# Adding all mixture outputs on VectorE ahead of the first scan, and writing the skip term with ScalarE

## What is computed

```python
x = x + 0.5 * moe(LN(x))        # 8 experts, 2 chosen per token, hidden 512
x = x + mamba(LN(x)) + mamba'(flip(LN(x)))   # two directions, own weights
x = x + 0.5 * moe(LN(x))

def step(h, inp):                # per token t, channel d (256), state n (16)
    u_t, d_t, b_t, c_t = inp
    dA = jnp.exp(d_t[:, :, None] * A)
    h = h * dA + (d_t * u_t)[:, :, None] * b_t[:, None, :]
    return h, jnp.einsum('bdn,bn->bd', h, c_t)
y = scan(step) + xc * Dp         # xc * Dp is the skip term
y = (y * silu(z)) @ out_w.T
```

## Time and profile before

| | us |
|---|---|
| median of 3 runs | 2886.86 |
| lowest, highest | 2885.48, 2887.90 |
| the profiled execution | 2884.83 |
| its span, first to last instruction | 2883.0 |
| first mixture, 0 to 510 | 510 |
| between the mixture and the first scan, 510 to 558 | 48 |
| scan stage, 558 to 2323 | 1765 |
| second mixture and end, 2323 to 2883 | 560 |

### The profile page before, as it was taken

The page is one execution under the profiler, slowest core; times in us unless marked ns, Lnnn a source line. Parts: engine busy times, 40 slices in busy tenths (PEclk is TensorE's granted clock), DMA queues, the critical chain, the costliest instruction groups (busy, mean ns, idle before and its releaser), DMA issues.

```text
span 2883.0 us, 38519 instructions
## 1 busy us (share of the span) xinstructions
PE 2461.9 (85%) x11100; PEld 1556.7 (54%) x11100; DVE 2456.1 (85%) x3745; ACT 1583.6 (55%) x2776; POOL 2305.3 (80%) x1392
## 2 busy tenths in 40 slices
PE   4799999588898889889889889989988865999993
PEld 2699999343444444344344444434434435999993
DVE  6766666499999999999999999999999978666666
ACT  3355555466566566656656665665665541555551
POOL 1577777399999999999899999999998844777772
PEclk8899999899999999999999999999999987999996
DMA  7011112133333333233233333233323240111116
GB/s 226 14 49 49 49 49 49 61 101 100 97 106 103 96 106 101 92 107 102 94 105 106 97 103 106 95 100 107 100 92 99 97 136 5 45 49 49 49 49 192
DMA packets 159363, 254.75 MB, mean 88 GB/s; under 512 B 22114, under 2 KB 64002, under 8 KB 158594
## 3 DMA queue, kind: packets, MB, share of 16 engines
q1 hardware_dynamic: 140338, 209.21, 23.1%
q0 software_dynamic: 18464, 37.79, 4.9%
q10 hardware_dynamic: 432, 6.29, 0.5%
HBM read 219.65 MB, written 33.55 MB: 88 GB/s over the span
## 4 chain that ended last, share of the span: by engine, by line
DVE 29%; issue 21%; PE 16%; POOL 10%; ACT 5%; DMA 1%; POOLq 0%; DVEq 0%; SPq 0%
DVE buf L828 11%; PE bank L1342 7%; DVE bank L804 7%; DVE buf L819 6%; POOL buf L404 5%; ACT over L1069 2%; POOL token_outputs L414 2%; POOL buf L465 2%; PE bank L1338 2%; PE bank L1279 2%; PE bank L1287 2%; DVE buf L792 1%; PE bank L1193 1%; ACT L1035 1%; DVE X L727 1%
## 5 line engine op out<-in xcount | busy, mean ns | idle before, releaser
L465 POOL TENSOR_TENSOR buf<-buf 128x1024 f32<-128x1024 f32 x512 | 1203.4, 2362 | 140.0 <-DVE buf L828 114.8
L1342 PE MATMUL bank<-buf,id_sb 128*128 128x512 f32 x2048 | 1001.1, 618 | 105.8 <-POOL buf L465 100.8
L828 DVE TENSOR_TENSOR_SCAN buf<-over,bank 128x512 f32<-128x512 f32 x768 | 891.7, 1201 | 1.0
L1069 ACT ACTIVATE over<-wgu,negA 128x510 f32<-128x510 f32 x768 | 505.5, 711 | 470.4 <-DVE buf L828 429.8
L1342 PEld LDWEIGHTS bank<-buf,id_sb 128*128 128x128 f32 x2048 | 385.9, 195 | 538.9 <-issue 336.6
L804 DVE TENSOR_TENSOR bank<-wgu,bank 128x512 f32<-128x512 f32 x768 | 488.4, 681 | 6.6 <-PE bank L1329 4.1
L1212 PE MATMUL bank<-parts 128*128 128x256 f32 x3456 | 486.2, 291 | 3.2 <-issue 1.6
L1212 PEld LDWEIGHTS bank<-parts 128*128 128x128 f32 x3456 | 434.1, 192 | 7.1 <-issue 3.9
L414 POOL DMA_INDIRECT token_outputs<-buf,slot_out x288 | 292.8, 1017 | 110.2 <-issue 85.3
L404 POOL DMA_INDIRECT buf<-token_rows,slot_token x288 | 302.7, 1051 | 96.7 <-issue 90.4
L1329 PE MATMUL bank<-BCs,sel 104*128 104x512 f32 x384 | 271.9, 709 | 74.7 <-DVE bank L804 73.4
(11 more groups left out here) (158 smaller groups left out, 2403.0 us busy)
## 6 DMA issues: line engine op xcount, KB each, us to landing
buf<-state_rows SPq DMA_DIRECT2D x640, 256.0 KB, 3.2
token_rows<-buf SPq DMA_DIRECT2D x32, 256.0 KB, 2.3
y_pair<-token_outputs SPq DMA_DIRECT2D x16, 512.0 KB, 5.2
buf<-token_outputs SPq DMA_DIRECT2D x16, 512.0 KB, 5.0
buf<-token_rows,slot_token POOLq DMA_INDIRECT x288, 2.6
token_outputs<-buf,slot_out POOLq DMA_INDIRECT x288, 2.3
out<-X SPq DMA_DIRECT2D x16, 256.0 KB, 3.7
wgu<-wgT ACTq DMA_DIRECT2D x1, 2048.0 KB, 9.2
```

What stands on the lines that cost most here:

```text
L465: pool.tensor_tensor(hC[:, b, :].rearrange("p (c w) -> p c w", c=C), hs[:, b, :].rearrange("p (c w) -> p c w", c=C), Cs[:, b, :].unsqueeze ...
L828: V.tensor_tensor_scan(hs[:, b, w], dA[:, b, c, :, :].rearrange("p s t -> p (s t)"), bank[c], 0.0, ALU.mult, ALU.add).then_inc(s[f"scan_do ...
L1069: ins = A.activation(dA[:, n % R, c, :, 1:], delta[r][:, c * W:(c + 1) * W].rearrange("p (s t) -> p s t", s=S)[:, :, 1:], ACT.Exp, scale=n ...
L1342: ins = M.matmul(bank[4 + c], id_sb[:, :], hC[:, n % R, c * W:(c + 1) * W], start=False, stop=(n == NS - 1), skip_group_check=True)
```

## The change

Four things are changed.

- The loads of mixture outputs of all 16 groups of four tiles are made ahead of the first scan, eleven before SP's first store of B and C rows and five after it (`EARLY` = 11), into a ring of four buffers `y_pre`, which is the down weights' tile `wd_sb` under another shape.
- DVE adds them with the instruction that it uses after the second mixture, eight per group (`combine_early`): group 0, then pair 0's layer norm, groups 1 to 10, `split_lo(0, 0)`, groups 11 to 14, `step_size(0, 0)`, group 15 (`MIDDLE` = 15), and the first product. ACT's `scale_outputs` and POOL's `combine` are gone.
- The down weights are loaded a second time, at the end of unit 1, by SP.
- The skip term is written by ACT into the y banks at n = 2 of each unit, after the gate (`skip`, two instructions with Dp as the scale), and PE's first sum waits for it (`skip_done`) in place of the two skip products. Two products ahead of the first scan open the banks once (`y_opened`). `skip_sb` and `y_pair` are gone.

```diff
+EARLY, MIDDLE = 11, 15
+        y_pre = wd_sb[:, :, :].rearrange("p (b t k) d -> p b t k d", t=G, k=2)
...
             outputs_there(0)
-            sp.dma_start(y_pair[:, :, :, :], y_rows(0)).then_inc(s["y_pair_in"], DMA)
...
+            def load_early(g):
+                wait(sp, s["comb_done"], g - 3)
+                sp.dma_start(y_pre[:, g % 4, :, :, :], y_rows(g)).then_inc(s[f"y_pre{g % 4}"], DMA)
+
+            for g in range(EARLY):
+                load_early(g)
...
             store_rows(0, 0)
-            load_pair(1)
+            for g in range(EARLY, NG):
+                load_early(g)
...
+                        if u == 1 and n == NS - 1:
+                            sp.wait_ge(s["comb_done"], NG)
+                            sp.dma_start(wd_sb[:, :, :], wdT).then_inc(s["loaded_w"], DMA)
...
-            combine(0, 0)
-            combine(0, 1)
             rstd(0)
...
+            def combine_early(g):
+                dve.wait_ge(s[f"y_pre{g % 4}"], (g // 4 + 1) * DMA)
+                combine(0, g, y_pre[:, g % 4, :, :, :])
...
+            combine_early(0)
             layernorm(0)
+            for g in range(1, EARLY):
+                combine_early(g)
             split_lo(0, 0)
+            for g in range(EARLY, MIDDLE):
+                combine_early(g)
             step_size(0, 0)
+            for g in range(MIDDLE, NG):
+                combine_early(g)
             product(0, 0, 0)
...
+            def skip(u, r):
+
+                if isinstance(u, int) and u == 0:
+                    act.wait_ge(s["y_opened"], C)
+                wait(act, s["gated"], u)
+                act.wait_ge(s["act_pre"], done(ACT_PRE, f"xc1_{r}", u // 2))
+                for c in range(C):
+                    ins = A.activation(bank[4 + c], xc[r][:, c * W:(c + 1) * W], ACT.Copy,
+                                       scale=ch[:, r, c, DSK:DSK + 1])
+                ins.then_inc(s["skip_done"], 1)
...
+                        if n == ACT_AT["skip"]:
+                            skip(p * 2 + r, r)
...
                 if n == 0:
-                    wait(pe, s["gated"], p * 2 + r)
-                    for c in range(C):
-                        M.matmul(bank[4 + c], skip_sb[:, r, c, :], xc[r][:, c * W:(c + 1) * W],
-                                 start=True, stop=False, skip_group_check=True)
+                    pe.wait_ge(s["skip_done"], p * 2 + r + 1)
```

More of the change, by code:

```diff
@@ L43 @@
 DVE_AT = {"gate": 2, "stats": 5, "lo": 8, "size": 12}
-POOL_AT = {"first": 0, "second": 1, "rstd": 7, "du": 13}
-ACT_AT = {"silus": 4, "hi": 7, "res": 8, "parts": 10, "ln": 11, "xn": 12, "scale": 13, "xnT": 15}
+POOL_AT = {"rstd": 7, "du": 13}
+ACT_AT = {"skip": 2, "silus": 4, "hi": 7, "res": 8, "parts": 10, "ln": 11, "xn": 12, "xnT": 15}
 PE_AT = {"conv": 0, "z": 5, "xdbl": 6, "out": 7, "dt": 9, "xt": 13}
-SP_AT = {"pair": 3, "rows": 9}
+SP_AT = {"rows": 9}
+EARLY, MIDDLE = 11, 15
 NSTATE = 16
@@ L155, in macaron_kernel @@
         slot_token = sb("slot_token", [P, TILES * HT], I32)
-        y_pair = sb("y_pair", [P, G, 2, D])
         sel = sb("sel", [ROWS, BC], F32R)
@@ L344, in pair_rows @@
                             fetch_B(u, r, n + FETCH_B)
-                        if n == SP_AT["pair"] and r == 0 and not (last or isinstance(p, int) and p == NP - 2):
-                            load_pair(p + 2)
                         if n == SP_AT["rows"] and not (last and r == 1):
                             store_rows(u + 1, 1 - r)
+                        if u == 1 and n == NS - 1:
+                            sp.wait_ge(s["comb_done"], NG)
+                            sp.dma_start(wd_sb[:, :, :], wdT).then_inc(s["loaded_w"], DMA)
             store_rows(0, 0)
-            load_pair(1)
+            for g in range(EARLY, NG):
+                load_early(g)
             for n in range(FETCH_C):
@@ L475, in pair @@
                             product(p, r, n + MUL_LEAD)
-                        if r == 0 and not last:
-                            if n == POOL_AT["first"]:
-                                combine(p + 1, 0)
-                            if n == POOL_AT["second"]:
-                                combine(p + 1, 1)
-                            if n == POOL_AT["rstd"]:
-                                rstd(p + 1)
+                        if r == 0 and not last and n == POOL_AT["rstd"]:
+                            rstd(p + 1)
                         if n == POOL_AT["du"] and not (last and r == 1):
                             size_times_input(p + r, 1 - r)
-            def combine(p, k):
-                pool.wait_ge(s["y_scaled"], p + 1)
-                wait(pool, s["pair_added"], 2 * p + k)
-                pool.sem_inc(s["out_turn"], 1)
-                xt = X[:, bass.ds(p * G, G), :]
-                pool.tensor_tensor(xt, xt, y_pair[:, :, k, :], ALU.add).then_inc(s["pair_added"], 1)
             def size_times_input(p, r):
@@ L720, in moe, with combine @@
                 four(TILES // 4 - 1)
-            def combine(g, rows):
+            def combine(m, g, rows):
                 for k in range(2):
@@ L753, in _ @@
             chain(V.tensor_copy(dtp_parts[0][:, :, :], dtp_sb[:, :, :]))
[L754 to L758 removed]
+            V.tensor_tensor(dtp_parts[1][:, :, :], dtp_sb[:, :, :], dtp_parts[0][:, :, :].bitcast(F32),
+                            ALU.subtract).then_inc(s["parts_ready"], 1)
             for b in range(4):
@@ L1006, in normalise @@
                 ins.then_inc(s["act_norm"], 1)
-            def scale_outputs(p):
-                act.wait_ge(s["y_pair_in"], (p + 1) * DMA)
-                for t in range(G):
-                    for k in range(2):
-                        ins = A.activation(y_pair[:, t, k, :], y_pair[:, t, k, :], ACT.Copy,
-                                           scale=wt[:, k, p * G + t:p * G + t + 1])
-                ins.then_inc(s["y_scaled"], 1)
+            def skip(u, r):
[7 more added lines that the diff above has]
+                ins.then_inc(s["skip_done"], 1)
             def normT(p):
@@ L1108, in pair @@
                             log1pexp(pv, rv)
-                        if r == 1 and n == ACT_AT["scale"] and p + 2 < NP:
-                            scale_outputs(p + 2)
                         if r == 0 and not last:
@@ L1386, in _ @@
                          start=True, stop=True).then_inc(s["taps_spread"], 1)
+            for c in range(C):
+                M.matmul(bank[4 + c].rearrange("p (j d) -> p j d", j=G), ones_sb[:, :], id_sb[:, :].unsqueeze(1).broadcast_to([P, G, P]),
+                         start=True, stop=True).then_inc(s["y_opened"], 1)
             pe.wait_ge(s["taps_ready"], 1)
@@ L1392, in _ @@
             project_x(0, 0)
+            pe.wait_ge(s["parts_ready"], 1)
             project_dt(0, 0)
```

35 lines of the change are left out of this document (12 added, 23 removed).

## The result

| | us |
|---|---|
| before, median of 15 runs | 2885.75 |
| changed, median of 15 runs (lowest, highest) | 2891.65 (2889.47, 2893.35) |
| ratio, 95% interval | 1.0019 (1.0011 to 1.0027) |
| profiled span, before and after | 2883.0, 2888.4 |

The change costs 0.19%, where 2893.3 was forecast from a kernel of 2886.86 (ratio 1.0022): slower, by about as much as this kernel's measurement can tell from nothing. Two effects of opposite sign lie behind that.

What follows compares the result with a forecast made beforehand. DVE was taken to bound the scan stage, with nothing saturated ahead of the first scan. Profiled 2884.83 + 4.4 (start) + 2 (scan stage: -15 + 17) = 2891.2, or 2893.3 against the median of 2886.86; own range 2888 to 2901, wider 2875 to 2904.

Steps and rivals of the forecast that it cites:

- that case, 8 to 12 falls: Forecast's own case: 8 to 12 clock falls at the gates, start 2.6 to 8.2 us later, 2888 to 2901; chance 0.45.
- a start of +4.4: Ahead of the first scan: adds on DVE make the scans start 4.4 us later, bounds 2.6 to 8.2 us.
- not 0.50: At each gate: with the skip on ACT, PE's sums start 0.50 us earlier; -15 us over 30 gates, -20 to -8.
- six, not ten: PE's longer pause at the gates: 10 clock falls in 30, between 0 and 17; +17 us, between 0 and +30.
- predicted was +2: Scan stage as a whole: -15 us from the skip and +17 us from clock falls make +2 us.
- one wait of about 2 us at group 11: Sign ahead of the first scan: DVE busy from 521 us on, with this one wait, first product near 562.
- with group 15 beside POOL's product, in DVE's old wait: Before the first product: group 15 runs in DVE's old wait of 2.46 us; first product 3.7 us after `step_size` as before.
- an estimate of 6.6 us: Start if group 15 and POOL's product share a port and can't run side by side: 6.6 us later, not 4.4.
- What was taken at nothing: Scan stage: combine, scaling, second down-weights load (at most 3 us, once) and queued decay of state 6 at 0; end as before.
- the clock did not hold: Rival: the clock holds at the gates, so the skip's gain stands; 2876.3 us, chance 0.25.
- it did not fall at most gates: Rival: the clock falls at most gates, 17 falls costing 30 us; 2906.3 us, chance 0.12.
- a few falls only: Rival: five clock falls at the gates cost 9 us; 2885.3 us, no measurable difference, chance 0.18.

Runs made afterwards that it cites:

- the skip alone: The kernel before with only the skip term moved to ACT, the mixture adds left on POOL and ACT; ratio 0.9997.
- group 15 ahead: The changed kernel with group 15's adds on DVE ahead of `step_size` (`MIDDLE` = 16); ratio 1.0024 against the kernel before.
- the earlier loads: The changed kernel with 13 instead of 11 loads issued ahead of SP's first store of B and C rows; ratio 1.0015 against the kernel before.
- the skip on PE: The changed kernel with the skip term put back on PE, all 16 groups' adds staying on DVE; ratio 1.0024 against the kernel before.
- the zero product: The changed kernel with one product by a tile of zeros in PE's pause at the gate; ratio 0.999 against the kernel before.

## Why the prediction was right, point by point

The forecast was 2893.3 and the time is 2891.65, within the forecast's own range. The mechanisms were the ones named: a shorter chain, falls of the clock behind the longer pause, and a later start. But the condition of that case, 8 to 12 falls, did not come about; there were six. By the prediction's own prices (1.74 us for a fall) six falls and a start of +4.4 make 2886.9 - 15 + 10.4 + 4.4 = 2886.7, no measurable difference. The two terms were off by 2.6 and 4.5 us in opposite directions, so that the number came out within 2 us is in part luck.

**The skip on ACT.** ACT's pair takes 1.30 us (1.28 predicted) and the sums start 1.39 us behind the gate (1.38), where the earlier trace rows have 1.88. But the sums behind a pause reach their next instruction 3.54 us later (1129.32 to 1132.86), where behind no pause they take 3.43 (1134.79 to 1138.22), so 0.11 us is lost at once. The projection starts 1138.22 - 1127.93 = 10.29 us behind the gate's end, where it started 1021.46 - 1010.79 = 10.67 us behind it: 0.38 us earlier. And the chain from the gate to the bank scan is that much shorter: 641.07 - 622.04 = 19.03 us before, 648.53 - 629.88 = 18.65 us after. The intervals confirm it, 55.36 to 54.97. **0.38 us per gate, not 0.50**: 11.6 us, not 15. The prediction took PE's work behind the pause at the price of work without one. The kernel before paid nearly the same behind its pause of 0.71: four skip products took 1.82 us there, where half of 3.43 is 1.72. So this part did not leave PE with the skip, but passed on to the sums.

DVE's waits, one row of each kind:

```profile
648.53 2.43 DVE L809 TENSOR_TENSOR_SCAN buf<-bank,buf 128x256 f32<-128x256 f32 x4 [1.38 <-ACT bank L1081]
...
1197.04 1.29 DVE L794 TENSOR_TENSOR bank<-wgu,bank 128x512 f32<-128x512 f32 x2 [1.55 <-PE bank L1326]
1201.99 2.43 DVE L809 TENSOR_TENSOR_SCAN buf<-bank,buf 128x256 f32<-128x256 f32 x4 [1.42 <-ACT bank L1081]
```

Units with a layer norm show none without a fall, units without one 1.38 us. Together they are 31.7 us; 34 to 35 were predicted, for ten falls.

**The clock.** The pause is 2.04 us (2.03 predicted). A fall costs 56.67 - 54.97 = 1.70 us (1.74 predicted), and reaches the interval in full. That the price was right to 0.04 us came of reading it from one gate at the lower level. The number of falls was the weak step: **six, not ten**, so 10.2 us, not 17. Over the four kernels with this pause (the changed one, the skip alone, group 15 ahead, and the earlier loads) there were 6, 8, 6 and 7 falls in 30 gates, 27 in 120. The bracket from 5 in 56 (pauses of 1.2 to 1.5 us) to 9 in 16 (2.65 us) did hold it, and its middle didn't. In the changed kernel the next fall comes five units after the last, in one place four; with the skip alone it was two to five. The pauses are not all alike either: 68 of the 120 are 2.04 to 2.06 us long, with 25 of the falls, and 52 are 1.58 to 1.94, with 2. So the falls keep to the full pauses, and still only about a third of those has one. What sets the moment is open; no run here was made to tell.

The Trainium skill, TensorE: Matmul & The Clock Gate, Part 1, says that a gate passes either all or half of TensorE's clock pulses, by how busy the engine has been. The trace agrees: from 1184 to 1188 the granted clock was 1.00 until the fall at 1185.54 and 0.69 in the mean, which leaves 0.50 for the other 2.46 us, and the sums took 5.40 us in place of 3.70.

So the scan stage came to -11.6 + 10.2 = -1.4 us, and -2.5 with the long unit that before happened to have (56.71 and 55.63 in place of 55.36, 1.6 us) against two short excesses after (0.46 us); predicted was +2.

**The start.** Predicted +4.4 at the first product, measured +6.98. By its steps, all with 1.19 us of drift taken off the times after: the first add at 521.4 (521.2 predicted). Group 11's load is used at 550.4 (549.7). It was issued at 547.58 and took 4.0 us, against 3.9; but it was issued 0.6 us later than predicted. The layer norm had begun 0.5 us later than predicted, and POOL's four small operations of it take 2.57 us from the first start to the last end (526.68 to 529.25), where they took 1.93 in the trace of before (528.25 to 530.18); against that, the way from ACT's normalising to its copy of the B and C rows was 0.4 us shorter (17.27 us, and 17.71 before). The second POOL row above has 0.45 us; in the trace of before the same operation took 0.23, with DVE idle. The wait of 2.15 us was foreseen ("one wait of about 2 us at group 11"). Then comes `step_size` at 559.4 (558.6), which is 0.8 us of the miss of 2.6. Group 15 takes 4.40 us, not 2.23: 2.17 us more, of which DVE's old wait had some 0.4 us to give. So from the start of `step_size` to the first product it is 5.45 us and not 3.7, and these 1.75 us are the rest of the miss. **The step that failed is "with group 15 beside POOL's product, in DVE's old wait"**: I took the value without interference and left its opposite as a bound.

The rule cited there, the Trainium skill, SBUF — State Buffer, section "Who interferes with whom", led to an estimate of 6.6 us, and 6.98 was measured. The trace agrees with it: 4.40 against 2.23 us here and with the loads earlier, and 4.41 with the skip on PE and with the zero product, each time with one add of 2.44 us as long as POOL's product, while POOL's own product grew by 0.04 us. In the other direction it shows only in part. POOL's four small operations took 0.37, 0.45, 1.13 and 0.39 us in the changed kernel, and about the same in two others; with group 15 ahead and with the loads earlier, where the same adds run beside them, they took 0.37, 0.23, 1.04 and 0.20, so only the first was longer than the 0.24 of before. What decides there is open. Between the first product and the first gate 0.33 us come back, which is the shorter skip of the first unit, and leave 6.65 us.

**What was taken at nothing** stayed there: no new wait of POOL for rows after the second load of the down weights (the longest in 600 to 2325 us for such a row is 0.3 us), ACT's next decay starts behind a wait of 0.87 us for a scan, so the queued decay of state 6 was covered, and the end takes 597.47 us against 597.41.

**The sum.** -1.4 - 1.1 + 6.65 = +4.2 us by the stages, +5.9 between the medians (interval 3.2 to 7.8). The difference is less than what the end of the mixture drifts by. The rivals: the clock did not hold, and it did not fall at most gates; "a few falls only" asked for about five and had their number nearly right, but with 0.50 us gained at each gate and a start of +4.4 it came to 2885.3, no measurable difference. The errors of the two terms, 2.6 us too little at the start and 4.5 us too much in the scan stage, nearly cancelled.

## What to carry to other kernels

Before work is put into an engine's wait, ask whether the two that would then run side by side can do so: here eight adds, 2.23 us in all, went into a wait of 2.46 us, and the way to the first product became 1.75 us longer, since DVE stood still for as long as POOL worked. A shorter chain that leaves a longer pause on PE should be sent with something for PE to do in that pause: here, in the kernel with the skip on ACT alone, one product by zeros turned nothing into -0.4%. And before a chain is shortened by moving work between engines, look at what stands directly ahead of the awaited instruction on its own engine: two decays that nobody needed yet stood there, and letting the awaited ones past them was worth 27 us.

## What the runs showed of the hardware that was not expected

- Eight weighted adds on DVE with both inputs in SBUF take 4.40 us beside POOL's product of 2.39 us, and 2.23 us alone. The added time is in one add of 2.44 us, which ends with POOL's product; almost none is added to POOL's own.
- After a pause of 2.05 us with the clock granted in full, eight products take 3.54 us to the next one's start, and 3.43 without a pause. Behind a pause of 0.71 us the difference is the same, 0.1 us.
- A pause of PE at the gate was followed by a fall of the clock in 25 of 68 gates where it was 2.04 to 2.06 us long, and in 2 of 52 where it was 1.58 to 1.94. With pauses of 0.72 us or less none of 60 gates had a fall (before, and the adds alone), and with pauses of up to 1.20 us behind a zero product none of 120 (four kernels).
- ACT's plain write into a bank serves as the start of PE's accumulation: the sums added to it in all eight kernels with the skip on ACT, two writes of 128x512 taking 1.30 us. Each of these kernels had opened the banks once by a product; none was run without, so whether that is needed is not shown.
